# A two-layer graph network on one core: three radial networks in the prepare stage, and buffers of their own for the first receivers' tables

## What is computed

```python
# layer 0, per edge: emb is 8 Gaussians of the edge's length
h = silu(emb @ mlp_w0 + mlp_b0)
h = silu(h @ mlp_w1 + mlp_b1)
w = (h @ mlp_w2 + mlp_b2).reshape(-1, 4, 32)      # the radial network
ss, vv = (s @ W_up0)[senders], (v @ W_up1)[senders]
mid_s = concat([w0 * ss, w3 * dot(vv, Y1)])
mid_v = concat([w1 * ss * Y1, w2 * vv])
x = layernorm(x + out(segment_sum(mid, receivers)))
# layer 1, per edge, for its type t of four
h = relu(concat([x[src], x[dst]]) @ W1[t] + b1[t])
m = (h @ W2[t] + b2[t]) * sigmoid(concat(...) @ attn_w[t] + attn_b[t])
x_new = GRU(sum of m by dst, x) + x ; layernorm twice
```

## Time and profile before

| | us |
|---|---|
| three runs | 3151.82, 3176.6, 3148.94 |
| median | 3151.82 |
| the profiled execution's own time | 3156.88 |
| its span | 3155.2 |
| mean granted clock of PE | 0.77 of full |

### The profile page before, as it was taken

The page is one execution under the profiler, slowest core; times in us unless marked ns, Lnnn a source line. Parts: engine busy times, 40 slices in busy tenths (PEclk is TensorE's granted clock), DMA queues, the critical chain, the costliest instruction groups (busy, mean ns, idle before and its releaser), DMA issues. The chain is left out here.

```text
span 3155.2 us, 43900 instructions
## 1 busy us (share of the span) xinstructions
PE 2120.1 (67%) x10012; PEld 1630.4 (52%) x10012; DVE 1477.7 (47%) x3700; ACT 1326.8 (42%) x4413; POOL 1609.8 (51%) x1699
## 2 busy tenths in 40 slices
PE   5577888778787887878845655656555656565555
PEld 3355555555555555555624544545545645555444
DVE  5334434343433443434423435646555646465556
ACT  3255545555555565555613323333323333333332
POOL 4454555555555455554233455555545555555451
PEclk6677888888888788888858777777767767777677
DMA  6311212222222122221135443333333433333331
GB/s 188 86 42 38 56 50 61 53 59 52 52 60 57 48 61 53 62 57 48 46 100 141 130 108 81 84 88 83 85 80 77 97 76 89 79 89 83 74 85 41
DMA packets 222533, 236.66 MB, mean 75 GB/s; under 512 B 73191, under 2 KB 163471, under 8 KB 222349
## 3 DMA queue, kind: packets, MB, share of 16 engines
q0 software_dynamic: 53808, 112.80, 15.5%
q10 hardware_dynamic: 90192, 57.89, 7.2%
q1 hardware_dynamic: 78493, 65.53, 7.0%
HBM read 191.73 MB, written 44.31 MB: 75 GB/s over the span
## 5 line engine op out<-in xcount | busy, mean ns | idle before, releaser
L549 POOL DMA_INDIRECT gx<-node_d,idx x832 | 802.2, 964 | 684.3 <-DVEq L1041 410.7
L549 POOL DMA_INDIRECT gp<-p_tab_d,idx x832 | 790.1, 950 | 692.2 <-DMA idx<-p_idx_d 405.4
L849 PEld LDWEIGHTS ps_a<-hot,msg 128*128 128x128 f32 x3328 | 489.3, 230 | 252.8 <-issue 233.5
L849 PE MATMUL ps_a<-hot,msg 128*128 128x128 f32 x3328 | 521.7, 319 | 93.8 <-issue 53.1
L616 ACT ACTIVATE msg<-ws,y 128x32 f32<-128x32 f32 x2496 | 549.7, 310 | 5.4 <-DVE ws L595 4.1
L1669 PE MATMUL ps_e<-win,hot_x 128*128 128x129 f32 x1680 | 333.5, 370 | 272.2 <-DVE hid L1812 130.5
L1669 PEld LDWEIGHTS ps_e<-win,hot_x 128*128 128x128 f32 x1680 | 302.1, 274 | 297.0 <-issue 151.6
L1733 PE MATMUL ps_g<-hot,hid 128*128 128x128 f32 x1664 | 255.1, 307 | 105.8 <-issue 102.7
L1777 DVE TENSOR_TENSOR hot_x<-key_row,ps_s 128x1024 f32<-128x1024 bf16 x106 | 128.8, 1216 | 401.0 <-remote 360.8
L747 ACT ACTIVATE h<-ps_h,b 128x512 f32<-128x512 f32 x208 | 141.8, 682 | 401.0 <-remote 265.3
L1733 PEld LDWEIGHTS ps_g<-hot,hid 128*128 128x128 f32 x1664 | 244.7, 222 | 122.3 <-issue 115.6
(11 more groups left out here) (210 smaller groups left out, 2477.9 us busy)
## 6 DMA issues: line engine op xcount, KB each, us to landing
win<-q_tab_d ACTq DMA_DIRECT2D x416, 64.5 KB
key_row<-key_row_d ACTq DMA_DIRECT2D x102, 256.0 KB
gx<-node_d,idx POOLq DMA_INDIRECT x832
gp<-p_tab_d,idx POOLq DMA_INDIRECT x832
q_tab_d<-unit_area SPq DMA_DIRECT2D x51, 258.0 KB
p_tab_d<-acc SPq DMA_DIRECT2D x23, 516.0 KB
emb<-emb_d SPq DMA_DIRECT2D x104, 32.0 KB
gx<-in_x_t ACTq DMA_DIRECT2D x7, 448.0 KB, 7.0
```

The lines of the kernel that those rows point to most:

```text
L549: e.indirect_dma_start(out=buf[:, h, t, :], out_offset=None, in_=table, in_offset=bass.IndirectOffsetOnAxis(ap=idx[:, h, t:t + 1], axis=0) ...
L849: last = e.matmul(ps_a[:, h, b, :], msgs[h].tile(t, b), hot[:, h, t, :], start=t == 0, stop=t == TPS - 1)
```

## The change

**Radial networks.** The buffers and semaphores of the radial network (`h1`, `h2`, `ps_h`, `ps_x`, `ps_w`) are made by a new function `first_mlp` ahead of both stages, and `prepare` runs the network in the middle of its own work: all three parts of step 0, two of step 1 and the first of step 2. They read the embedding from SBUF, where `prepare` made it. `edges0` starts without them, and loads the embeddings of steps 3 and 4 at its start. `load_emb(j)` now loads step j+5 and waits for the first part of step j+3. A row of zeros is stored after the last embedding, since step 104 is now loaded too.

**Queues in prepare.** The stores of `p_idx`, `q_idx` and `key_row` go from SP's queue to ACT's, between and behind the `Silu` of the networks. The eight gathers of step 3 go from the end of `prepare` to the start of `edges0`.

**Layer 1.** The first four index columns of layer 1 are loaded at the start of `edges0`, into a buffer that both stages see. The first five chunks of the table are evicted to columns of `acc` of their own and stored in one transfer a chunk (`store_first`). The windows of step 0 are issued once chunk 0 is stored and those of step 1 once chunk 1 is. PE does the receivers of step 0 after three chunks, not five. DVE zeroes the area of these buffers only inside step 0, once all five are stored; that zeroing covers 7740 columns, where it covered 5536 before. ACT's first three rounds are written out, not looped. Some semaphores are merged.

```diff
 prepare
-                e.wait_ge(row_ok, 1)
-                e.dma_start(dram["key_row"], key_r).then_inc(row_st, 16)
-                e.wait_ge(idx_ok, 1)
-                e.dma_start(dram["p_idx"], p_idx).then_inc(stored, 16)
-                e.dma_start(dram["q_idx"], q_idx).then_inc(stored, 16)
-                e.wait_ge(stored, 16 * 2)
+                e.dma_start(dram["emb"][STEPS], k["zero"][0:2 * NB, :]).then_inc(stored, 16)
+                e.wait_ge(stored, 16 * 3)
...
                     e.activation(emb[:, span], emb[:, span], ACT.Exp, scale=-0.5).then_inc(exp_ok, 1)
+                e.preload_act_table(ACT.Silu)
+                layer0_silu(e, w, mlp, 1, 1)
+                layer0_silu(e, w, mlp, 2, 1)
+                e.wait_ge(idx_ok, 1)
+                e.dma_start(dram["p_idx"], p_idx).then_inc(stored, 16)
+                e.dma_start(dram["q_idx"], q_idx).then_inc(stored, 16)
+                layer0_silu(e, w, mlp, 1, 2)
+                layer0_silu(e, w, mlp, 2, 2)
+                e.wait_ge(row_ok, 1)
+                e.dma_start(dram["key_row"], key_r).then_inc(row_st, 16)
...
-                for u in range(SLOTS):
+                for u in range(SLOTS - 1):
                     e.wait_ge(w["idx_in"][u], 16)
...
+                e.wait_ge(mlp_ok, 1)
+                e.wait_ge(s_own, SPC)
+                e.wait_ge(tab_ok, NG)
+                e.wait_ge(exp_ok, 1)
+                first(0)
+                layer0_second(e, w, mlp, 1)
+                layer0_third(e, w, mlp, 0, 1)
+                first(1)
+                layer0_second(e, w, mlp, 2)
+                e.wait_ge(mlp["h2_ok"], 2)
+                first(2)
 edges0
                 def load_emb(j, h):
-                    e.wait_ge(h1_mm, j + 1)
-                    e.dma_start(emb[:, h, :], dram["emb"][bass.ds(j + 2, 1)].rearrange("s r n -> (s r) n"))\
+                    e.wait_ge(h1_mm, j + 4)
+                    e.dma_start(emb[:, h, :], dram["emb"][bass.ds(j + 5, 1)].rearrange("s r n -> (s r) n"))\
                         .then_inc(emb_in[h], 16)
...
+                for u in range(SLOTS):
+                    e.dma_start(k["idx1"][:, u, :], dram["p_idx"][:, u * TPS:(u + 1) * TPS]).then_inc(k["idx_in1"][u], 16)
...
             def _(e):
+                e.wait_ge(idx_in[SLOTS - 1], 16)
+                e.sem_inc(gate, 1)
+                gather_step(e, idx, dram["node0"], gx, landed, SLOTS - 1)
                 gather_loop(e, idx, idx_in, dram["node0"], gx, landed, used, gate, first=1)
...
-                first(0, 16)
-                second(1)
-                third(0, 1)
-                first(1, 16)
-                second(2)
-                e.wait_ge(h2_ok, 2)
-                first(0, 32)
 edges1
+                def store_first(c):
+                    e.wait_ge(q_ev, 2 * CH * (c + 1) + 2)
+                    if c >= CH:
+                        e.wait_ge(q_first[c % CH], 16 * (c // CH))
+                    e.dma_start(q_g[:, c * CH:(c + 1) * CH, :], first_buf[:, c * CH:(c + 1) * CH, :])\
+                        .then_inc(q_first[c % CH], 16)
+                    next_xq(c)
...
-                store_table(0)
-                store_table(1)
-                first_windows(0)
-                store_table(2)
-                first_windows(1)
+                for c in range(2):
+                    store_first(c)
+                    e.wait_ge(q_first[c], 16)
+                    load_windows(e, regs, c, c)
...
                 def table_out(c, s):
-                    e.wait_ge(q_st[s], c * 16 + 16)
+                    to = first_buf[:, c * CH + s, :] if c < AHEAD else q_buf[:, s, :]
+                    if c >= AHEAD:
+                        e.wait_ge(q_st[s], (c - AHEAD) * 16 + 16)
...
-                for c in range(AHEAD):
+                for c in range(CH):
                     for s in range(CH):
                         q_table(0, c, s)
                 e.wait_ge(hx_ok, 1)
                 e.wait_ge(win_in[0], 16 * PPS)
                 for q in range(NQ):
                     receivers(0, q)
+                for c in range(CH, AHEAD):
+                    for s in range(CH):
+                        q_table(0, c, s)
...
                         edge_rows(i, u, not first or u > 0)
+                        if first and u == 0:
+                            for c in range(CH):
+                                e.wait_ge(q_first[c], 16 * ((AHEAD - 1 - c) // CH + 1))
+                            e.memset(k["acc"][:, 2 * NACC0:max(first_end, nodes["end"])], 0.0).then_inc(zero_ok, 1)
+                            e.wait_ge(zero_ok, 4)
...
-                e.memset(k["acc"][:, 2 * NACC0:nodes["end"]], 0.0).then_inc(zero_ok, 1)
-                e.wait_ge(zero_ok, 4)
+                e.wait_ge(zero_ok, 3)
```

158 lines of the change are left out of this document (85 added, 73 removed).

## The result

| | before | changed |
|---|---|---|
| median of 15 runs, us | 3156.19 | 3193.39 |
| lowest to highest, us | 3144.7 to 3178.9 | 3164.5 to 3225.35 |
| span of the profiled execution, us | 3155.2 | 3191.7 |

The ratio is 1.0097 (95% interval 1.0065 to 1.0129): the change makes the kernel 1% slower, where 3130 us, a gain, was forecast. The ratio leaves out slow runs, three of the changed kernel (3212.57, 3215.23 and 3225.35 us). 3193 lies outside the range and beyond the rival that was to end on the slower side (3186).

The account below looks back on a forecast made before the run. The prediction took edges0 to go by PE, with pauses, and prepare by its gathers. Terms of -6, -12, 0 and -4 us summed to -22 us, taking the median from 3151.8 to 3130 us, range 3106 to 3152.

Parts of the forecast that it names:

- What moves through SP's queue in edges0: Loop of edges0: the index load may go out up to a step later, but DVE isn't late; term 0.
- The sign that was set for it: In edges0: a step of over 14.6 us would show the forecast wrong.
- The slower rival: In edges0: index load tied to PE's step makes more double batches, up to 7 us each; 3186 us, chance 0.08.
- End of prepare: End of prepare: the zeroing ends last, at 96 us instead of the stage's 102; -6 us, between 0 and -10.
- First steps of edges0: Start of edges0: step 1's weights come 13.6 us after the stage's start, not 28.7; -12 us, between -15 and -8.
- Start of edges1: Start of edges1: step 0 comes sooner, but the later zeroing holds step 1; -4 us, between 0 and -15.
- the first rival: Layer 1: batches of steps 4 and 5 come apart, one 16.06 us pause less; 3114 us, chance 0.25.
- What bounds the kernel: Whole kernel: gathers bound prepare, PE with pauses bounds edges0, where PE is busy 79%.

Follow-up runs that it names:

- experiment 5: Changed kernel with SP loading the index of step j+4 first, then the embedding of step j+3 after the first part of step j+1: 3128.6 us, ratio 0.9898.
- experiments 4 and 11: Kernel before with layer 1 as changed: 3128.5 us; kernel before with an always fulfilled wait between fourth and fifth gather of each edges0 batch: 3143.1 us.
- a_idx_first: Changed kernel with SP issuing the index load of step j+4 ahead of the embedding load of step j+5 in edges0: 3189.6 us, ratio 1.0142.
- experiment 6: Changed kernel with the eight gathers of step 3 back at the end of prepare: 3192.6 us, ratio 1.0111.

## Why the prediction was wrong

**The step that failed** is "What moves through SP's queue in edges0", with its "Term: 0". It held that an index up to one step late costs nothing, since the gather still has three steps. That argument was about the deadline of the data, and the data were never late: among DVE's waits in the changed kernel, 300 to 1580 us, none is for a gather. What the term left out is that the arrival of the index also sets when POOL's batch starts, and with it whether two batches run into each other and the other engines stand still. It measured +61.6 us, and experiment 5 takes it back to +2.4 (1440.0 - 1437.6) by rearranging SP's loads alone. The sign that was set for it came too: 14.95 us a step, where over 14.6 was to show the forecast wrong.

**The slower rival** had the right effect in the right place, more double batches in `edges0` by the index released with PE's step, and was given a chance of 0.08. In these 80 steps joined batches went from 7 to 19. Its argument against ("the load waits at most one step") was the same slip. Its price of 7 us each is of the right size for the sum (12 x 7 = 84 against 55 in 80 steps), but experiments 4 and 11 have 11 and 14 joined batches, 4 and 7 more than before, for 8 and 13 us in 80 steps (14.36 and 14.42 us a step against 14.26), under 2 us each. So the count of joined batches doesn't carry the time by itself; a fixed price for each is not shown.

**End of prepare**: -12 us, where -6 was forecast. The zeroing ended last, as said, but at 90.0 and not at 96. `key_row` was issued at 75.00 and not at 85.7, and over half of these 10.7 us are luck. ACT's two `Exp`, ahead of which both kernels do the same work, ran here as

```profile
56.41 5.84 ACT L411 ACTIVATE acc<-acc 128x3072 f32<-128x3072 f32 x2
```

and ended at 62.25, 6.3 us sooner than in the earlier trace rows. From 25 to 55 us PE's granted clock was 0.61 here and 0.50, the lower of its two levels throughout, in the profile before, so what it makes for ACT there was done sooner. The start of the `Exp` lies between 54.9 and 63.7 us in the eight traces with the old `prepare`, and between 54.2 and 62.8 in the twelve with the new one. In the trace of a_idx_first, with the same new `prepare` and a clock of 0.50 there, they started at 62.68 as before, and the zeroing ended at 97.7: -4 us. The rest of the 10.7 us is of the change: the networks start once the first of the two `Exp` is done, and the index stores on ACT's queue cost no time that can be seen between the `Silu`. The landing took longer than either value weighed (86.44 - 75.00 = 11.4 us until the zeroing, against 3 and 9.2). The forecast let the stage close with the zeroing for its 96 and 3.5 us behind it for its upper bound; it closed with it.

**First steps of edges0**: -16 us, where -12 was forecast (step 1's `ws` 12.7 us after the stage's start, and 13.6 was said). The 3 us for step 3's gathers were not paid: from the first `ws` to that of step 1 it takes 9.4 us with them alongside, and 10.2 us without them in experiment 6. Both starts together gave 28.0 us, and 18 were forecast. In a_idx_first, whose `Exp` start as in the earlier trace rows, they gave 20.4 us (`ws` of step 1 at 110.3): the two terms were nearly right, and the rest is the luck of `prepare`.

**Start of edges1**: the mechanism was right in each part. `hid` of step 0 came 17 us sooner, the zeroing took 6.51 us (6.5 said), and `hid` of step 1 came where it was before; -1.8 us to that mark (-4 said). The premise of the first rival came true as well: the batches of steps 4 and 5 came apart (POOL idle for 9.1 us between them, where it was 0.3), and at the `hid` of step 20 the changed kernel was 8 us ahead of the one before, counted from the `ws` of step 103. By the end it was 3 us behind, so the gain that the rival forecast did not stay. POOL beside the zeroing:

```profile
1705.30 0.95 POOL L599 DMA_INDIRECT gp<-p_tab_d,idx  x1 [28.67 <-DMA idx<-p_idx_d]
1706.55 0.94 POOL L599 DMA_INDIRECT gp<-p_tab_d,idx  x1 [0.30 <-issue]
```

The box "DVE blocks DMA" of the Trainium skill, SBUF — State Buffer, tells of GpSimd being locked out of writing descriptors while DVE runs a 2-port perf-mode operation. The MEMSET ran from 1700.30 to 1706.81, and a gather began and ended in it in its usual 0.95 us once its index was in; with the earlier trace rows that makes two places where a MEMSET held no gather back.

**What bounds the kernel**: I read "PE, with pauses", and then treated the pauses as a given. They were the larger matter: 14.26 us a step before, 12.6 with batches at an even distance, 10.0 in the jobs where nothing pauses.

**What stays open.** Whether the held index alone makes the loss or the later embedding load has a part in it (experiment 5 moved both). Whether the hold costs anything once the batches are cut. Why the same event, PE's first part, gives an even rhythm as a hold on POOL and the pattern of three steps as a hold on SP's load; the traces differ in the 2.6 us between the index's issue and the batch, and in SP's other transfers in the same queue, and neither was varied. And what makes the engines stop beside long batches at 3150 us and not at 2277 us: the same kind of program, the same gathers at the same 1.25 us. Each job ran on a chip of its own, so that it is the chip and not the time is not shown either. That the engines lack instructions in a pause has nothing for it: among the transfers from 949 to 971 us in the changed kernel there is none of an instruction queue. What kind of event ends the pause ("remote") the profile doesn't say.
